# Two attentions of a decoder: the order of the last output rows and the last head's values

## The reference, cut to what matters

```python
# L1_attn: 32 heads of 128, 8 key/value heads, 512 cached keys + 256 new ones
attn = softmax(einsum('bhld,bhtd->bhlt', q, k_full) / sqrt(128))
out  = einsum('bhlt,bhtd->bhld', attn, v_full)            # values of every head
x = x + out.reshape(b, l, 32 * 128) @ wo.T
# L1_xattn: 16 heads of 96, 4 key/value heads, 512 context keys + 256 own ones
x = x + xattn(layernorm(x), ctx) @ Wo.T
# L1_ffn: 8 experts, two chosen for each token by a gate
x = x + experts(layernorm(x))
```

## Time and profile before

| | |
|---|---|
| time, median of 3 runs (lowest, highest) | 1210.74 us (1204.33, 1213.07) |
| span of the profiled execution | 1210.8 us |
| TensorE busy | 1107.5 us, 91% |
| VectorE busy | 877.0 us, 72% |
| ScalarE busy | 604.6 us, 50% |
| GpSimd busy | 489.2 us, 40% |
| mean granted TensorE clock | 0.967 of full speed |
| end of the first attention (last units to first product of the next stage) | about 787 to 815 us |
| end of the second attention (the same) | about 1081 to 1116 us |

### The profile page before, as it was taken

One profiled execution on the slowest core, in us unless ns is written; L12 is line 12 of the kernel. 1 busy time (PEld: TensorE's weight loads), 2 busy tenths in 40 slices (PEclk: granted clock), 3 DMA queues, 4 the chain that ended last, 5 costly groups with the idle time before them and its releaser, 6 DMA issues.

```text
span 1210.8 us, 17596 instructions
## 1 busy us (share of the span) xinstructions
PE 1107.5 (91%) x5819; PEld 886.3 (73%) x5826; DVE 877.0 (72%) x1480; ACT 604.6 (50%) x1231; POOL 489.2 (40%) x360
## 2 busy tenths in 40 slices
PE   3867867898999999999999999979899999988998
PEld 2433433377888888888888888768798888877887
DVE  7999988779868777777868687656666666655344
ACT  2523443345656566565656565643665656551110
POOL 1370000124546555454646464532665655440000
PEclk9988988899999999999999999989999999997999
DMA  9363144220020010111010100141103030210231
GB/s 324 119 217 139 53 161 156 74 83 18 18 66 19 24 58 22 52 30 52 21 53 22 51 0 25 51 138 40 47 18 90 18 89 1 81 71 0 70 104 69
DMA packets 41812, 83.10 MB, mean 69 GB/s; under 512 B 10211, under 2 KB 18916, under 8 KB 38564
## 3 DMA queue, kind: packets, MB, share of 16 engines
q1 hardware_dynamic: 40164, 77.24, 19.8%
q0 software_dynamic: 1600, 5.24, 1.4%
HBM read 71.59 MB, written 10.22 MB: 68 GB/s over the span
## 4 chain that ended last, share of the span: by engine, by line
PE 77%; DVE 12%; ACT 4%; issue 4%; POOL 2%; DMA 1%; SPq 0%; ACTq 0%; DVEq 0%; POOLq 0%
PE PS L1829 21%; PE PS L1831 20%; PE PS L1830 20%; PE PS L1960 9%; PE PS L1792 1%; PE PS L1636 1%; ACT arena L951 1%; PE PS L1618 1%; ACT PTH L966 1%; DMA arena<-in_ctx 1%; PE PS L1776 1%; DVE arena L1263 1%; PE PS L1687 1%; PE PS L2088 1%; PE PS L1803 1%
## 5 line engine op out<-in xcount | busy, mean ns | idle before, releaser
L673 POOL TENSOR_TENSOR arena<-arena,rsum 128x768 f32<-128x768 f32 x192 | 283.3, 1476 | 373.0 <-DVE rsum L1434 373.0
L966 ACT ACTIVATE PTH<-PS 128x384 fp32r<-128x384 f32 x384 | 167.9, 489 | 249.7 <-PE PS L1960 249.3
L1429 DVE TENSOR_REDUCE nmax<-PS 128x1 f32<-128x768 f32 x192 | 183.0, 953 | 115.9 <-PE PS L1831 114.6
L1479 DVE TENSOR_TENSOR PTL<-PS,PTH 128x384 fp32r<-128x384 f32 x384 | 194.4, 547 | 7.8 <-ACT PTH L966 7.2
L951 ACT ACTIVATE arena<-PS,nmax 128x768 f32<-128x768 f32 x192 | 174.2, 907 | 40.2 <-DVE nmax L1429 40.1
L1960 PE MATMUL PS<-identf,arena 128*128 128x128 f32 x1152 | 158.4, 273 | 7.3 <-DVE PTL L1479 6.0
L1960 PEld LDWEIGHTS PS<-identf,arena 128*128 128x128 f32 x1152 | 130.1, 140 | 10.9 <-issue 6.2
L1829 PE MATMUL PS<-PTH,VSH 128*128 128x512 f32 (+1 forms) x198 | 81.0, 409 | 2.5 <-DVE OTL L1450 2.0
L658 POOL TENSOR_TENSOR WQL<-arena,WQH 128x512 fp32r<-128x512 f32 x44 | 57.2, 1302 | 60.3 <-ACT WQH L735 60.3
L1829 PE MATMUL PS<-WOH,OTH 128*128 128x512 f32 (+1 forms) x180 | 75.0, 416 | 2.1 <-DVE OTL L1450 2.0
L1831 PE MATMUL PS<-PTH,VSL 128*128 128x512 f32 (+1 forms) x198 | 76.4, 386 | 0.0
(11 more groups left out here) (270 smaller groups left out, 2544.4 us busy)
## 6 DMA issues: line engine op xcount, KB each, us to landing
arena<-in_wo SPq DMA_DIRECT2D x12, 1024.0 KB, 4.8
arena<-in_wq SPq DMA_DIRECT2D x44, 256.0 KB, 2.6
arena<-in_expert_w SPq DMA_DIRECT2D x8, 1024.0 KB, 4.8
arena<-in_wgu SPq DMA_DIRECT2D x11, 512.0 KB, 5.1
arena<-v_dram SPq DMA_DIRECT2D x8, 384.0 KB, 3.4
arena<-in_wd SPq DMA_DIRECT2D x4, 704.0 KB, 4.9
arena<-in_ctx SPq DMA_DIRECT2D x4, 512.0 KB, 4.1
arena<-in_ctx_t SPq DMA_DIRECT2D x2, 1024.0 KB, 10.8
```

The lines of the kernel that those rows point to most:

```text
L673: pool.tensor_tensor(PR[:, u % 4, :], PR[:, u % 4, :], rsum[:, u % 4:u % 4 + 1].broadcast_to([P, KEYS]), ALU.mult).then_inc(s["pn_ready"], 1)
L966: act.activation(fr(PTH[:, (u // 4) % 2, 3 * half:3 * half + 3, u % 4 * P:(u % 4 + 1) * P]), bank(B_PT[half])[:, 0:3 * P].rearrange("p (k ...
L1429: dve.tensor_reduce(nmax[:, slot:slot + 1], SC[pair][:, 0:KEYS], AX.X, ALU.max, negate=True)\
L1479: dve.tensor_tensor(fr(PTL[:, (u // 4) % 2, ks, cols]), bank(B_PT[half])[:, 0:3 * P].rearrange("p (k c) -> p k c", k=3), PTH[:, (u // 4) % ...
```

## The change

The list of TensorE's products at the end of each attention has the same matmuls in another order. Row tiles 0 and 1 get heads 0 to 2, then half 0 of the last head's values is made; row tile 2 gets heads 0 to 2; then row tiles 0 and 1 get head 3 and are complete. Then comes half 1 of the values, then heads 0 and 1 of row tile 3, the wait for half 1, head 3 of row tile 2, and heads 2 and 3 of row tile 3. On VectorE the additions and statistics of row tiles 0 and 1 move ahead of the low part of half 1. ScalarE, GpSimd and SP keep their lists.

```diff
@@ VectorE, end of attention
                     dve.wait_ge(s[hi], count)
                     dve.tensor_tensor(fr(OTL[0:hd, GH - 1, cols]), bank(LAST_OT[half])[0:hd, cols],
                                       OTH[0:hd, GH - 1, cols], ALU.subtract).then_inc(s[ev], 1)
-                for r in range(RT):
-                    output_added(first + groups - 1, r, LAST_BANKS[r])
-                    dve.wait_ge(s["y_added"], RT * (first + groups - 1) + r + 1)
-                    row_stats(5 if first else 4, r)
+                    for r in range(half * RT // 2, (half + 1) * RT // 2):
+                        output_added(first + groups - 1, r, LAST_BANKS[r])
+                        dve.wait_ge(s["y_added"], RT * (first + groups - 1) + r + 1)
+                        row_stats(5 if first else 4, r)
@@ TensorE, last_head_values
-                def last_head_values(g):
+                def last_head_values(g, half):
 
                     j = GH - 1
-                    pe.wait_ge(s["pt_out1"], UNITS * (g + 1))
-                    pe.wait_ge(s["pt_out0"], UNITS * (g + 1))
-                    pe.wait_ge(s["ot_ev"], GH * g + j)
-                    for half in range(2):
-                        cols = slice(half * S, (half + 1) * S)
+                    if half == 0:
+                        pe.wait_ge(s["pt_out1"], UNITS * (g + 1))
+                        pe.wait_ge(s["pt_out0"], UNITS * (g + 1))
+                        pe.wait_ge(s["ot_ev"], GH * g + j)
+                    cols = slice(half * S, (half + 1) * S)
...
@@ TensorE, end of attention
                 pe.wait_ge(s["y_added"], RT * g)
-                for r in range(RT):
+                for r in range(2):
                     project_out(g, r, LAST_BANKS[r], range(GH - 1), last=True)
-                last_head_values(g)
+                last_head_values(g, 0)
+                project_out(g, 2, LAST_BANKS[2], range(GH - 1), last=True)
                 pe.wait_ge(s["ot_half_ev"], 2 if first else 1)
-                for r in range(RT):
-                    if r == RT // 2:
-                        pe.wait_ge(s["ot_ev"], GH * (g + 1))
+                for r in range(2):
                     project_out(g, r, LAST_BANKS[r], range(GH - 1, GH), last=True)
+                last_head_values(g, 1)
+                project_out(g, 3, LAST_BANKS[3], range(2), last=True)
+                pe.wait_ge(s["ot_ev"], GH * (g + 1))
+                project_out(g, 2, LAST_BANKS[2], range(GH - 1, GH), last=True)
+                project_out(g, 3, LAST_BANKS[3], range(2, GH), last=True)
```

More of the change, by code:

```diff
@@ L1874, in head_values @@
                         mm.then_inc(s["ot_psum"], 1)
-                def last_head_values(g):
+                def last_head_values(g, half):
                     j = GH - 1
-                    pe.wait_ge(s["pt_out1"], UNITS * (g + 1))
-                    pe.wait_ge(s["pt_out0"], UNITS * (g + 1))
-                    pe.wait_ge(s["ot_ev"], GH * g + j)
-                    for half in range(2):
-                        cols = slice(half * S, (half + 1) * S)
[L1884 to L1892, removed]
+                    if half == 0:
[3 more added lines that the diff above has]
+                    cols = slice(half * S, (half + 1) * S)
+                    for k in range(KK):
+                        if hd == HD1:
+                            mm = product(bank(LAST_OT[half])[:, cols], VSH[:, k, :], VSL[:, k, :],
+                                         PTH[:, j % 2, k, cols], PTL[:, j % 2, k, cols], k == 0, k == KK - 1)
+                        else:
+                            mm = product(bank(LAST_OT[half])[0:hd, cols], VH2[:, half * KK + k, :],
+                                         values_lo(half * KK + k), PTH[:, j % 2, k, cols], PTL[:, j % 2, k, cols],
+                                         k == 0, k == KK - 1)
+                    mm.then_inc(s[("ot_half", "ot_psum")[half]], 1)
                 def project_out(g, r, bk, heads=range(GH), last=False):
```

## The result

The changed kernel took 1204.77 us (median of 4 runs, 1202.54 to 1206.46) beside 1211.9 us for the kernel before: ratio 0.9946, 95% interval 0.992 to 0.9972. So it is faster by 0.5 to 0.7%, 6.5 to 8.6 us, which is clear of the scatter and less than 1%. The forecast was 1205 us and 5.6 us.

The account below looks back on a forecast made before the run. TensorE was taken to bound the kernel except at both attention ends, where VectorE's adds and statistics hold the chain; gains of 2.42 + 2.38 + 0.75 = 5.55 us from 1210.8 gave 1205 us, range 1199 to 1212.

Parts of the forecast that it names:

- VectorE's tail bounds the ends: Both attention ends: VectorE's adds and statistics hold the chain while TensorE idles, 6.30 us of them in the first end.
- TensorE's schedule in the first end: First attention's end: the same 84 products reordered from 788.58, ending at about 804.2 as before, if no new wait bites.
- The three waits: First end, TensorE waiting for head 3's last low parts and both half splits: margins 3.2, 1.07 and 0.37 us, no cost.
- Gain of the first end: First attention's end: the last tile's add starts at 804.25 instead of 806.67, gaining 2.42 us.
- Gain of the second end: Second attention's end: the last statistics start at 1100.83 instead of 1103.21, gaining 2.38 us.
- margin of 0.6 us: Second end: half 0's low part ready at about 1092.28, behind the second EXWL on VectorE, and wanted at 1092.88.
- Rival B: Both ends: the thin margins fail, stalling up to 1 us in each end; 1207 to 1209 us, chance 18%.
- rival A: Both ends: the shorter idle stretch keeps TensorE's clock up; 1195 us, or about 1201 with one end, chance 12%.
- The clock: Transposes at both ends run less at half rate after shorter idle time: 0.75 us gained, bounds 0 and 2.8.
- part of rival A in brackets: Both ends: the shorter idle stretch lets the full clock come back earlier, instead of keeping it up.
- D: Both ends: the order changes nothing because something else paces VectorE's list; 1210 to 1212 us, chance 6%.
- C: Both ends: weights ScalarE rounds ahead of half 0 land late, stalling TensorE; 1214 us if 5 us late, chance 4%.

Follow-up runs that it names:

- EXWL out of the way: Changed kernel with VectorE's second EXWL moved from ahead of half 0's low part to behind the transposed rows' low parts: ratio 0.9924, repeated 0.994.
- the kernel without the cover: Changed kernel with heads 0 to 2 of row tile 2 moved behind head 3 of tiles 0 and 1: ratio 0.9957.
- idle matmuls: Kernel before plus unused 512-column matmuls behind each attention's last closing product and behind the transposes: ratio 0.996.

## Why the prediction was right, point by point

**VectorE's tail bounds the ends.** Right. TensorE's order without VectorE's gives 0.72 us of 2.42 in the first end, VectorE's without TensorE's makes the row later by 1.43, and the sum needs both.

**TensorE's schedule in the first end.** Right: tile 0's add was placed 9.37 us behind the first closing product and came at 9.36, the low part of half 1 at 12.61 (came 12.61), the last add at 15.67 (15.66). The three waits bite nowhere there. Two slips stand in the working and carry nothing: the 6.30 us stand behind the add of tile 0 at 802.24, not behind 801.89, and the banks change nine times in each end in the new order as in the old, not four times more, so that the 0 taken for it follows from the lists.

**Gain of the first end.** 2.42 predicted, 2.42 measured.

**Gain of the second end.** 2.38 predicted. Measured with EXWL out of the way 2.38; in the changed kernel 1.18 and 1.05 (19.89 less 18.71 and 18.84), because the margin of 0.6 us did not hold. That margin was worked out from an execution in which the first 18 products ran partly at half clock; at full clock TensorE gets to the wait 1.5 us earlier, EXWL does not, and 0.91 to 1.04 us of waiting appear. Rival B, with a chance of 18%, was right for this end. The rows held the warning: in the earlier trace rows the 18 products take 5.79 us, and I used that for rival A but not for the margin.

**The clock.** Mis-sized. I took 0.75 us, from the transposes alone, and left the products behind them at nothing. In the first profile of the changed kernel the transposes gave 0.58 and 0.57 us (3.68 and 3.67 to 3.10), and behind them the key products 1.51 and the expert products about 0.5: 3.2 us. The part of rival A in brackets, that half clock ends earlier, took place, though the clock did fall. Its sentence that half clock begins behind a stretch of over 4.8 us is not what the rows say: it begins inside that stretch, 2.9 and 4.0 us behind the last product. With the new order alone in four profiles half clock in the first end was 10.2, 6.8, 3.4 and 3.4 us (a fifth had 3.4 twice, and the kernel without the cover none), with the old order and the full 4.9 us of idle time 13.7 in both. In the Trainium skill, TensorE: Matmul & The Clock Gate, section Why this matters for your kernels, stands the rule to avoid idle gaps between bursts of matmuls; the filled idle time in the kernel before, worth 4.8 us, agrees. I had treated what follows a gap as all or nothing, and in these profiles it comes by degrees.

**The sum.** 2.4 + 1.2 + 3.2 = 6.8 us of traced gains against 5.55 predicted: the second end's order was 1.2 too large, the clock 2.4 too small. Three more terms belong to single executions and close the account at 6.6: 0.90 gained ahead of the ends, 1.57 gained because the first closing products of the second end ran at full clock (21.46 less 19.89), 2.65 lost between the ends. This last one is clock too. The stretch from the first key product to the first closing product of the second end (the 1.51 on the key products included) took 265.4 us in the three profiles that have no half clock there (the second one of the changed kernel is among them), and over all thirteen 0.43 us more for each us of half clock: before had 6.1 us of it and took 268.2, the first profile of the changed kernel 9.6 and 269.3. The old order with idle matmuls has half clock there as well (861.4 to 864.8), so it is not peculiar to the new order; whether the change makes it more frequent is not shown.

The nearness of 1204.77 to the forecast of 1205 is in part luck. The two wrong terms have opposite signs, and the sum was taken from a span of 1210.8 as if it were the time of the run, which was 1213.1.

**The rivals.** D is refuted. A had its part in brackets, and B was right for the second end. C's mechanism exists, and a landing later by 1.2 us cost 1.2 us in one profile, but it came with the idle matmuls only, and no kernel with it was slower than before.

## What to carry to other kernels

When the last engine of a stage has a list of its own behind the last product, complete some of the output early enough for that list to run beside the remaining products. Reorder both engines: here neither order alone was a gain. Work the margins of the new waits out at the faster of the two clocks of TensorE too, since elementwise work does not slow down with it (normalising took 2.13 us at either clock), and look for weight preparation queued in order ahead of the new short step. An idle stretch of TensorE can cost twice, in itself and in the products behind it.

## What the runs showed of the hardware

TensorE's idle time of 2.5 us was followed by half clock of 0 (without the cover) to 10.2 us in the first end, and idle time filled with unused matmuls (gaps of 0.22 to 0.56 us left) by none in three profiles. With these gaps filled in the second end, the gate's 32 matmuls of 8 columns took 3.7 to 4.6 us in place of 6.97, but in all three of these kernels half clock followed, among their last or just behind them. And one elementwise subtraction on VectorE (96x512, 0.69 us elsewhere) took 3.88 us when GpSimd's subtraction of 128x1536 (3.62 us) ran beside it, and ended 0.56 us behind that one, in the changed kernel as before:

```profile
817.36 3.88 DVE L1550 TENSOR_TENSOR EKL<-arena,EKH 96x512 fp32r<-96x512 f32 x1
```

```profile
817.06 3.62 POOL L706 TENSOR_TENSOR WV2L<-arena,WV2H 128x1536 fp32r<-128x1536 f32 x1 [10.75 <-DVE EKL L1539]
```
